# A mixture-of-experts layer on one core: tile rows scaled by their share and added by the scatter into a DRAM buffer that holds the residual

## The reference

```
x = x + attn(layernorm(x));  x = x + xattn(layernorm(x), ctx_512);  x = x + ffn(layernorm(x))

gate_logits = einsum('bsd,de->bse', x, gate_kernel)
top_k_weights, top_k_indices = top_k(gate_logits, 2);  top_k_weights = softmax(top_k_weights)
inter = silu(x @ w0[e]) * (x @ w1[e])                 # 256 -> 512, for every expert e
out = sum over e of combine[.., e] * (inter @ wo[e])  # 512 -> 256
```

## Time and profile before

| | us |
|---|---|
| median of 3 runs | 564.37 |
| lowest, highest | 560.82, 571.93 |
| the profiled execution's own time | 561.27 |
| its span, first to last instruction | 559.5 |

### The profile page before, as it was taken

One profiled execution on the slowest core, in us unless ns is written; L12 is line 12 of the kernel. 1 busy time (PEld: TensorE's weight loads), 2 busy tenths in 40 slices (PEclk: granted clock), 3 DMA queues, 4 the chain that ended last, 5 costly groups with the idle time before them and its releaser, 6 DMA issues. The chain is left out here.

```text
span 559.5 us, 11805 instructions
## 1 busy us (share of the span) xinstructions
PE 491.8 (88%) x4163; PEld 419.0 (75%) x4164; DVE 339.7 (61%) x749; ACT 323.3 (58%) x762; POOL 144.0 (26%) x141
## 2 busy tenths in 40 slices
PE   2989999999899999999989799998507999999960
PEld 1778888888898888888689677776405888888850
DVE  5376666666725666666566376666652666666654
ACT  4477777788416777777662388887203444444430
POOL 5110000013000000000000438998011455555530
PEclk9999999999899999999999899999857999999995
DMA  9411111111100112110000033442221344444527
GB/s 264 160 59 57 56 56 56 56 57 57 39 1 20 57 57 56 56 56 0 1 1 2 2 101 127 147 131 102 76 94 51 119 169 156 151 159 158 165 76 225
DMA packets 24001, 48.05 MB, mean 86 GB/s; under 512 B 2960, under 2 KB 11168, under 8 KB 23968
## 3 DMA queue, kind: packets, MB, share of 16 engines
q1 hardware_dynamic: 21120, 41.17, 22.9%
q0 software_dynamic: 2240, 6.04, 3.1%
q10 hardware_dynamic: 608, 0.39, 0.3%
HBM read 42.48 MB, written 5.11 MB: 85 GB/s over the span
## 5 line engine op out<-in xcount | busy, mean ns | idle before, releaser
L651 PE MATMUL psum<-a_xt_hi,a_qk_hi 128*128 128x512 f32 x128 | 54.8, 428 | 1.4 <-DVE a_xt_lo L508 1.4
L570 DVE COPY a_weights_t<-psum 64x256 f32<-64x256 f32 x32 | 13.7, 428 | 63.5 <-PE psum L766 63.5
L1391 POOL DMA_INDIRECT picks_dram<-x_wout,e_pick_row x23 | 38.7, 1683 | 52.3 <-DVE x_wout L1554 52.3
L651 PE MATMUL psum<-a_xt_lo,a_qk_hi 128*128 128x512 f32 x128 | 51.7, 404 | 0.0
L651 PE MATMUL psum<-a_xt_hi,a_qk_lo 128*128 128x512 f32 x128 | 50.8, 397 | 0.0
L967 ACT ACTIVATE x_probs<-psum,x_neg_max 128x128 f32<-128x128 f32 x128 | 45.3, 375 | 8.1 <-DVE x_neg_max L1024 8.1
L1432 ACT ACTIVATE e_inner_hi<-psum 128x512 fp32r<-128x512 f32 x23 | 13.7, 598 | 57.9 <-PE psum L1614 57.9
L896 POOL MEMSET x_mask<- 128x512 bf16 x1 | 0.5, 524 | 172.3 <-POOLq L248 172.3
L1605 PE MATMUL psum<-expert_w_hi,e_x_hi 128*128 x92 | 39.2, 426 | 2.2 <-DVE e_x_lo L1532 2.2
L936 POOL TENSOR_TENSOR expert_w_lo<-x_xn_t,expert_w_hi 128x1024 fp32r<-128x1024 f32 x16 | 37.7, 2355 | 1.3
L780 PE MATMUL psum<-a_weights_t,a_v 64*128 64x64 f32 x256 | 34.9, 276 | 3.4 <-issue 2.5
(11 more groups left out here) (232 smaller groups left out, 1486.3 us busy)
## 6 DMA issues: line engine op xcount, KB each, us to landing
x_k_t<-in_expert_wo SPq DMA_DIRECT2D x23, 512.0 KB
a_qk_raw<-in_wqk SPq DMA_DIRECT2D x32, 256.0 KB, 2.6
x_xn_t<-in_expert_w SPq DMA_DIRECT2D x16, 512.0 KB, 3.8
a_wv_raw<-in_wv SPq DMA_DIRECT2D x17, 256.0 KB, 2.8
x_sb<-in_x SPq DMA_DIRECT2D x2, 512.0 KB, 5.1
x_k_t<-in_wo SPq DMA_DIRECT2D x1, 1024.0 KB, 10.5
x_v<-in_wo SPq DMA_DIRECT2D x1, 1024.0 KB, 13.1
xn_dram<-xn SPq DMA_DIRECT2D x1, 1024.0 KB, 4.4
```

Of the source, the lines that this page charges most:

```text
L570: dve.tensor_copy(weights_t[SEG:P, :, 0:2, :], t_ps[SEG:P, :, 0:2, :]).then_inc(wt_ready, 1)
L651: last = pe.matmul(out, pick_l(left[a], k), pick_r(right[b], k), start=start and n == 0, stop=n == 3 * KD - 1, skip_group_check=not start)
L1391: pool.indirect_dma_start(out=picks_dram, out_offset=bass.IndirectOffsetOnAxis(ap=pick_row[:, tile:tile + 1], axis=0), in_=y_rows[:, slot, ...
```

## The change

The DRAM buffer of the picks is replaced by `sums_dram`, with one row for each token and 128 spare rows. SyncE fills it with x_sb ahead of the tiles (and the spare rows with one block of x_sb). Each tile's rows are multiplied by their shares while VectorE copies them from PSUM, and the scatter adds them to the row of their token (`compute_op=ALU.add`). As two picks of one token lie in different tiles, each scatter waits until the one before has landed. The rows' shares (`row_share`, one number per row and tile) come from 48 further matmuls with the one-hot matrices, on shares cut into three bfloat16 parts. At the end four DMAs copy sums_dram to the output. Two scratch tiles of the route now lie in `c.v`, and VectorE's loop over the tiles is written out.

```diff
+            sp.dma_start(sums_dram[0:B * P, :].rearrange("(b p) d -> p b d", p=P), c.x_sb[:, :, :]).then_inc(sums_begun, 16)
+            sp.dma_start(sums_dram[B * P:(B + 1) * P, :], c.x_sb[:, 0, :]).then_inc(sums_begun, 16)
             sp.wait_ge(owner_known, 1)
...
             for slot in range(2):
                 sp.wait_ge(y_stored[slot], 16 * ((TILES + 1 - slot) // 2))
-            picks = picks_dram[0:PICKS * P, :].rearrange("(k b p) d -> p k b d", k=TOPK, b=B)
-            for b in range(B):
-                for k in range(TOPK):
-                    sp.dma_start(picked[k][:, b, :], picks[:, k, b, :]).then_inc(gathered[b], 16)
-            for b in range(B):
-                sp.wait_ge(mixed, TOPK * (b - b % 2) + 3 + b % 2)
-                sp.dma_start(out[b], c.x_sb[:, b, :]).then_inc(out_stored, 16)
-            sp.wait_ge(out_stored, 16 * B)
+            for b in range(0, B, 2):
+                sp.dma_start(out[b:b + 2].rearrange("b p d -> (b p) d"), sums_dram[b * P:(b + 2) * P, :]).then_inc(out_stored, 16)
+            sp.wait_ge(out_stored, 16 * (B // 2))
...
             def store(tile):
                 slot = tile % 2
                 pool.wait_ge(y_ready, tile + 1)
-                pool.indirect_dma_start(out=picks_dram, out_offset=bass.IndirectOffsetOnAxis(ap=pick_row[:, tile:tile + 1], axis=0),
-                                        in_=y_rows[:, slot, :], in_offset=None).then_inc(y_stored[slot], 16)
+                if tile > 0:
+                    pool.wait_ge(y_stored[1 - slot], 16 * ((tile + 1) // 2))
+                pool.indirect_dma_start(out=sums_dram, out_offset=bass.IndirectOffsetOnAxis(ap=sum_row[:, tile:tile + 1], axis=0),
+                                        in_=y_rows[:, slot, :], in_offset=None, compute_op=ALU.add).then_inc(y_stored[slot], 16)
...
             pool.wait_ge(picks_known, 1)
+            pool.wait_ge(sums_begun, 32)
...
-            chained(dve.tensor_tensor(spare[:, :], spare[:, :], spare_row[:, :], ALU.mult))
-            chained(dve.tensor_tensor(spare[:, :], spare[:, :], pick[:, :], ALU.add))
-            dve.tensor_copy(pick_row[:, :], spare[:, :]).then_inc(picks_known, 1)
+            chained(dve.scalar_tensor_tensor(out=spare[:, :], in0=spare[:, :], scalar=spare_row[:, :], in1=token_f[:, :],
+                                             op0=ALU.mult, op1=ALU.add))
+            dve.tensor_copy(sum_row[:, :], spare[:, :]).then_inc(picks_known, 1)
+
+            shares = share[:, :, :].rearrange("p k b -> p (k b)")
+            chained(dve.tensor_copy(share_part[:, 0, :], shares))
+            chained(dve.tensor_tensor(share_rest[:, :], shares, share_part[:, 0, :], ALU.subtract))
+            chained(dve.tensor_copy(share_part[:, 1, :], share_rest[:, :]))
+            chained(dve.tensor_tensor(share_part[:, 2, :], share_rest[:, :], share_part[:, 1, :], ALU.subtract))
+            for part in range(3):
+                last = dve.tensor_tensor(in_share[:, :, part, :], in_tile[:, :, 2, :],
+                                         share_part[:, part, :].unsqueeze(2).to_broadcast([P, PICKS, TILES]), ALU.mult)
+            last.then_inc(in_share_ready, 1)
...
             wo_rest(0, 0)
+            dve.wait_ge(row_share_done, 1)
+            chained(dve.tensor_copy(row_share[:, :], share_ps))
             gated(0, 0)
...
-                dve.tensor_copy(y_rows[:, slot, :], y_ps[slot]).then_inc(y_ready, 1)
+                dve.tensor_scalar(y_rows[:, slot, :], y_ps[slot], row_share[:, tile:tile + 1], None, ALU.mult).then_inc(y_ready, 1)
...
             columns(1, 1, 0, False)
+            pe.wait_ge(in_share_ready, 1)
+            for n in range(PICKS):
+                for part in range(3):
+                    last = pe.matmul(share_ps, row_hot[:, n, :], in_share[:, n, part, :],
+                                     start=n == 0 and part == 0, stop=n == PICKS - 1 and part == 2)
+            last.then_inc(row_share_done, 1)
```

More of the change, by code:

```diff
@@ L1234, with expert_phase @@
 EW, OW = NE_WIDTH, KM * D
-def expert_phase(c, xn_dram, picks_dram, out):
+def expert_phase(c, xn_dram, sums_dram, out):
     nc = c.nc
@@ L1253, in expert_phase @@
     tile_start = sb("e_tile_start", [P, TILES + 1], F32)
-    spare_row = sb("e_spare_row", [P, TILES], F32)
+    spare_row = sb("e_spare_row", [P, 1], F32)
     ones = sb("e_ones", [P, P], BF16)
@@ L1265, in expert_phase @@
     share = sb("e_share", [P, TOPK, B], F32)
-    n_over = sb("e_n_over", [P, NE, NE], F32)
+    n_over = c.v[:, B - 1, 0:NE * NE].rearrange("p (e n) -> p e n", e=NE)
     n_tiles = sb("e_n_tiles", [P, NE], F32)
@@ L1272, in expert_phase @@
     row_f = sb("e_row_f", [P, TOPK, B], F32)
-    reached = sb("e_reached", [P, PICKS, TILES + 1], F32)
+    scratch = c.v[:, :, :].rearrange("p b d -> p (b d)")
+    reached = scratch[:, 0:PICKS * (TILES + 1)].rearrange("p (n t) -> p n t", n=PICKS)
     in_tile = sb("e_in_tile", [P, PICKS, 3, TILES], BF16)
@@ L1282, in expert_phase @@
     token_row = sb("e_token_row", [P, TILES], U32)
-    pick_row = sb("e_pick_row", [P, TILES], U32)
+    sum_row = sb("e_sum_row", [P, TILES], U32)
+    share_rest = sb("e_share_rest", [P, PICKS], F32)
+    share_part = sb("e_share_part", [P, 3, PICKS], BF16)
+    in_share = sb("e_in_share", [P, PICKS, 3, TILES], BF16)
+    row_share = sb("e_row_share", [P, TILES], F32)
     ended = sb("e_ended", [1, TILES, NE], F32)
@@ L1304, in expert_phase @@
     invert_ps = c.bank[2][:, 0:3 * TILES].rearrange("p (q t) -> p q t", q=3)
+    share_ps = c.bank[3][:, D:D + TILES]
     sem = c.sem
@@ L1318, in expert_phase @@
     t_done, t_ready, t_lo_ready, y_done, y_ready = sem("e_t_done"), sem("e_t_ready"), sem("e_t_lo_ready"), sem("e_y_done"), sem("e_y_ready")
-    gathered = [sem(f"e_gathered{i}") for i in range(B)]
-    mixed, out_stored = sem("e_mixed"), sem("e_out_stored")
+    in_share_ready, row_share_done = sem("e_in_share_ready"), sem("e_row_share_done")
+    sums_begun, out_stored = sem("e_sums_begun"), sem("e_out_stored")
     def tiles(eng, step):
@@ L1455, in _ @@
             chained(dve.tensor_scalar(tile_start[:, :], iota[:, 0:TILES + 1], float(P), None, ALU.mult))
-            dve.tensor_scalar(spare_row[:, :], tile_start[:, 0:TILES], iota[:, P:P + 1], float(PICKS * P), ALU.add, ALU.add)
+            dve.tensor_scalar(spare_row[:, :], iota[:, P:P + 1], float(B * P), None, ALU.add)
             for b in range(B):
@@ L1553, in step @@
                 wait_past(dve, y_stored[slot], pair * 16)
-                dve.tensor_copy(y_rows[:, slot, :], y_ps[slot]).then_inc(y_ready, 1)
+                dve.tensor_scalar(y_rows[:, slot, :], y_ps[slot], row_share[:, tile:tile + 1], None, ALU.mult).then_inc(y_ready, 1)
                 if more(left, 1):
                     wo_rest(tile + 1, 1 - slot)
-            tiles(dve, step)
-            for b in range(0, B, 2):
-                for k in range(TOPK):
-                    for i in range(2):
-                        if k == 0:
-                            dve.wait_ge(gathered[b + i], 16 * TOPK)
-                        else:
-                            dve.wait_ge(mixed, TOPK * b + i + 1)
-                        dve.scalar_tensor_tensor(out=c.x_sb[:, b + i, :], in0=picked[k][:, b + i, :], scalar=share[:, k, b + i:b + i + 1],
-                                                 in1=c.x_sb[:, b + i, :], op0=ALU.mult, op1=ALU.add).then_inc(mixed, 1)
+            for tile in range(TILES):
+                step(tile, tile % 2, tile // 2, TILES - 1 - tile)
         @block.tensor
@@ L1665, in decoder_layer @@
         cross_phase(c)
-        expert_phase(c, xn_dram, picks_dram, out)
+        expert_phase(c, xn_dram, sums_dram, out)
 def kernel(x, ctx_512, L0_attn_Wq, L0_attn_Wk, L0_attn_Wv, L0_attn_Wo, L0_attn_betas, L0_xattn_Wq, L0_xattn_Wkv_expand,
```

3 lines of the change are left out of this document (1 added, 2 removed).

## The result

| | before | changed |
|---|---|---|
| median of 4 runs each, same chip, us | 565.5 | 573.32 |
| lowest, highest | 560.82, 571.93 | 571.62, 574.84 |
| profiled execution's own time, span | 561.27, 559.5 | 574.84, 573.1 |

The ratio is 1.0182, 95% interval 1.0136 to 1.0228; it compares fast executions alone, and 571.93 is a slow one, so it is not the ratio of the two medians. The forecast was 557.3, within 2% and if anything a little faster; the kernel became slower. The measured 573.32 lies just inside the range (551 to 574), on the side of its slower rival.

The account below looks back on a forecast made before the run. TensorE was taken to bound the expert loop, with a two-tile chain through scatter and gather equally long and an unhidden 14.05 us tail. 561.27 - 9.05 + 0.8 + 3.7 + 0.55 = 557.3 us; range 551 to 574.

Parts of the forecast that it names:

- its slower rival: Loop, GpSimd ahead of the scatter: the adding scatter is slow and its own wait binds; 582.8 us at e = 3.0; chance 0.17.
- end, landing to end: Tail after the last scatter's landing: four DRAM-to-DRAM copies take 5.0 us in place of 14.05, saving 9.05.
- last scatter's extra landing (e): Last scatter: adding also reads 128 rows of 1 KB; extra time 0.8 us, bounds 0 and 3.0.
- loop, bytes ahead of the gather: Loop: the scatter's extra 128 KB read lands each gather 0.39 us later, 5.10 per tile against 4.92; +3.7 us.
- loop, the new wait: GpSimd, ahead of each scatter: wait for the previous landing is long met while e stays under 1.77; 0 us.
- head: Before the loop: VectorE's added operations +0.3 and TensorE's 48 matmuls +0.25, together +0.55 us, bounds 0 and 3.1.
- its sign of being wrong: Scatter and end: accumulate's landing over 4.9 us, or the four copies taking far more than 5.
- The first rival: Loop, GpSimd ahead of the scatter: slow adding scatter, its wait binds, pace 3.15 + e; 582.8 us at e = 3.0; chance 0.17.
- The third rival: Loop, GpSimd: descriptor writing grows from 0.97 to 1.46 us, pace 5.35 per tile, whole 562.1 us; chance 0.13.
- The forecast's own range: Whole kernel: 552 (tail 4.4, half the loop's cost, head 0) to 563 us (e = 3.0 at the end alone, head 3.1).
- the fourth rival: End: the DRAM-to-DRAM copy is half as fast, 4.3 us over the sum, whole 561.6 us; chance 0.08.
- The scaling of y: Loop, VectorE: the copy from PSUM becomes a multiplication, at most 0.02 us more per tile; counted as 0.

Follow-up runs that it names:

- the second buffer's kernel: Changed kernel, odd tiles adding to a second DRAM buffer and no wait for the previous scatter's landing: 566.21 us against 563.73 for the kernel before, ratio 1.0038.
- the halved issues: Kernel before with the gather ahead of the scatter, and 8 loads and 4 stores at the end instead of 16 and 8: ratio 0.9986.

## Why the prediction was wrong

| step | forecast | measured |
|---|---|---|
| end, landing to end | -9.05 | -7.4 |
| last scatter's extra landing (e) | +0.8 | +1.24 |
| loop, bytes ahead of the gather | +3.7 | with the longer descriptors +8.3; bytes 0.12 of 0.79 |
| loop, the new wait | 0 | +7.7 |
| head | +0.55 | -0.1 |
| start of the expert phase | not in the sum | +3.9 in this execution |

**The step that failed is "the loop, the new wait: 0".** The prediction gave this wait cover until e = 1.77, from 3.15 + e < 4.92, and took e = 0.8 from the scatter's own bytes. The first scatter of the loop starts 0.28 after its y, like every scatter before, and lands after 6.16: e is 3.0, the wait binds, and the landing is over the 4.9 that the prediction named as its sign of being wrong. The next y was ready at 444.50, and its scatter began at 446.81.

What was missing in the inequality is, first, the load of expert_wo. The prediction let it stand in the gather's way but not in the scatter's. The 3.15 is the landing of a scatter whose packets go ahead of the load's; the adding one's go behind. With the load cut to an eighth e is 1.4 at the same place. Second, the restart: after the landing 0.76 more pass before the scatter starts (the expectations' 0.73 is its longest piece in the chain), where the row of before for a released y, 0.28 from the end of the copy (470.70) to the scatter (470.98), had suggested little and the prediction had counted nothing. With it the limit is 4.92 - 0.76 - 3.15 = 1.01. Third, the ring: what the scatter waits for also delays the gather behind it and then TensorE, so the wait isn't absorbed but is part of the pace.

The first rival named this mechanism and place, and even e = 3.0. Its pace of 3.15 + e = 6.15 did not come, since a scatter that starts late after its y has a shorter landing: the median landing is 4.7. With that and the restart the pace is 4.67 + 0.76 = 5.43, against 106.95 / 22 = 4.86 before: 12.5 us in 22 tiles. The landings that are longer than the median make the rest of the 16.0; the three longest (6.16, 5.95, 5.85) are those of the scatters that start within 0.75 of their y. The experiments show it from several sides. The landing wait removed gives 7.7 back, the gather put ahead 12.9, the addition removed 14.7.

**e itself** was 0.8 for the last scatter and measured 1.24 (3.66 from start to the copies' issue against 2.42). In the loop it was 3.0 for the first scatter and 1.55 in the median. The queue's packets are 4448 against 2240 of before, with 46 indirect DMAs in each, so every scatter makes 96 more. The last scatter alone, 562.7 to 566.7 in slices of 0.1 us as in the earlier trace rows:

```profile
GB/s 0 0 0 0 0 0 0 0 0 0 0 0 0 0 0 0 0 0 0 0 0 10 113 41 92 184 102 31 92 225 205 154 62 0 0 0 0 0 0 0
DMA packets 144, 0.13 MB, mean 33 GB/s; under 512 B 16, under 2 KB 144, under 8 KB 144
```

The plain one moved its 0.13 MB in five slices and 32 packets of 4 KB, this one in twelve slices and 128 packets of 1 KB. Its first packet starts 2.11 after the scatter's start, before 1.54; from the first packet to the end of the last it takes 1.19, before 0.52. So of the 1.24, 0.57 is the longer writing (1.55 on GpSimd in place of 0.97) and 0.67 the slower transfer. The Trainium skill's rule cited in the prediction ("Collectives: The Full Stack", "The bandwidth ceiling": half the rate, for two source reads, which the page gives for a reduce-scatter) would make e 0.5. The transfer, at 0.44 of the plain one's rate, lies near it, but the 1.24 does not agree with it as a price for a scatter this small; whether the second read or the smaller packets slow the transfer isn't shown.

**The third rival** (0.13) holds as to its cause: 0.97 to 1.55 is more than the 0.49 it assumed, and on the chain of the second buffer's kernel it is 0.60. But it and the first rival were priced as alternatives, and they came together. The longer writing is part of e and also pushes the gather. By themselves they give 8.3 (second buffer) and 7.7 more with the wait, and no case of the prediction had the two together. The forecast's own range was also mis-added: its terms give 554.3 and 562.0 and not 552 and 563, which changes nothing here. The bytes' 0.39 was a queue's worth of time put where only 0.12 shows.

The other rule of the Trainium skill cited there ("SBUF — State Buffer", "Who interferes with whom": a two-input operation of VectorE leaves the descriptors' side of the shared port alone, which the page marks as inferred) can be held against more rows now. With e_wo_lo beside it the scatter took 1.72 without and 2.31 with the addition, without it 0.97 and 1.55; the overhead is 0.75 and 0.76. The rule does not agree with the trace, and the forecast had gone by the trace.

**The end** went as said but by less. Of the 9.05, 7.4 came. The 5.0 was taken from a store out of SBUF; the four copies took 6.65. That is 1.65 over, under half of the 4.3 that the fourth rival assumed, and a single copy takes 5.8. The old end was not long by its 24 issues, as the halved issues show; that it was long by its bytes is what is left, and no run tests it.

**The head** cost nothing. The chain there, against the earlier trace rows:

```profile
431.01 1.43 PE L1649 MATMUL psum<-e_in_share,e_row_hot 128*128 128x23 bf16 x48
...
432.63 0.49 PE L1612 MATMUL psum<-expert_w_hi,e_x_hi 128*128 x1 [0.19 <-issue]
...
435.37 0.66 PE L1621 MATMUL psum<-ident,xn 128*128 128x128 f32 x4 [1.08 <-DVE xn L1542]
```

The 48 matmuls took 1.43 to 1.62, not 2.7 to 3.9, and fill the gap in which TensorE waited anyway. From the first gather's start (418.60, before 414.76) the first product's transposes stand at 16.77, before at 16.88. The scaling of y takes 0.48 for 0.42, so +0.06 a tile and not the 0.02 at most; it is one link of the 10.60 above.

## What to carry to other kernels

A wait "long met" has to be priced with what else is on the queues when the DMA's packets come, and with everything between the landing and the next start. Here the adding scatter lands after 3.7 us alone and after 6.16 behind a 512 KB load that was issued later, and 0.76 of restart came on top. When a DMA gets slower, ask first what stands behind it in the same engine's queue: moving the gather ahead of the adding scatter gave back 12.9 of 16.0 us and cost nothing. And two mechanisms that share a cause (a longer DMA that is both waited for and in the way) are priced together, not offered as alternatives. Their gains do not simply add up either: the wait removed gave 7.7, the gather put ahead 12.9, and both 14.8.

## What the runs showed of the hardware

- An adding scatter of 128 rows of 1 KB: 1.55 us of GpSimd against 0.97, 3.7 to landing with nothing beside it against 2.40, 4.1 to 5.1 in the median in these loops, 144 packets where the overwriting one has 48 for the same bytes.
- A 512 KB load of SyncE's queue, issued 1.6 us after the adding scatter's start, had nearly all its packets through first: the scatter landed after 6.16, and after 4.53 beside a 64 KB load.
- Two semaphore waits ahead of an indirect DMA on GpSimd, one for VectorE and one for a DMA's landing. With the landing's wait last, the DMA starts 0.73 to 0.77 us after the landing where that binds (the changed kernel, the gather ahead, the small loads), and 0.28 after VectorE's release where the landing is long past (the plain scatter with its wait kept). With the landing's wait first it starts 0.27 after the landing (the four kernels with the waits exchanged). The reason stays open.
- A copy of 1 MB from DRAM to DRAM took 6.2 to 6.9 us to the end in four DMAs over these kernels, 6.5 both in pieces of 16 KB and in rows of 1 KB in the same kernel, and 5.8 in one DMA (one execution).
